# A fused attention and LayerNorm kernel: P times V in halves on neighbouring batches, a ring of eight units, scores copied in front of the transposition, LayerNorm's scale and shift on VectorE

## The chip, the cores and the metric

The kernel runs on one core of a Trainium2 chip. The metric is device time in microseconds of one launch that handles all 16 images. The engines are TensorE (PE; PEld is its weight load), VectorE (DVE), ScalarE (ACT), GpSimd (POOL) and SyncE (SP), which issues most transfers.

## The reference, cut to what matters

```python
x_seq = x.reshape(16, 900, 512)                # 16 images of 30 x 30 positions, float32
q, k, v = x_seq @ w + b                        # each split into 8 heads of 64 columns
scores = einsum('bhqd,bhkd->bhqk', q, k) / 8 + spatial_bias[|dh| + |dw|]
attn = softmax(scores)
ctx = einsum('bhqk,bhkd->bhqd', attn, v)       # back to (16, 900, 512)
resid = ctx @ wo + bo + x_seq
out = (resid - mean) * rsqrt(var + 1e-5) * gamma + beta
```

The bias depends only on the distance in the grid. The data are float32 throughout.

## The kernel before, in words

**Units.** A head pair (two heads of 64 columns, 128 partitions) is one of four per image. A *unit* is 60 queries (two rows of the grid) of one pair against all 900 keys: 15 units in a pair, 60 in an image (`UNITS`). The 900 keys lie as two halves of 450 on different partitions, so a unit is a tile of 128 partitions (4 blocks of 30 queries, padded to 32) by 2 heads by 450.

**What happens to a unit u.** Every engine's program is written out by hand as `body(im, u)`, run for u = 0 to 59 of each image in turn (`images`), and every engine runs strictly in that order. In the text "body 30" is an engine's instructions for u = 30. TensorE does its work in *batches* of two units, at even u.
- TensorE, batch u: the scores of units u+6 and u+7 (`scores`, L670; `AHEAD` is 6), into two PSUM places, one for even and one for odd units. The scores of a unit wait until the unit two before has been copied out.
- DVE, `biased_scores` (L919), in body u for unit u+6: adds the bias, finds the row minimum (the query weights are negated), and writes the result to `prob`, a ring of `RING` units in SBUF.
- ACT, `exponentials` (L787), body u, unit u+6: the exponential in place, with the row sum.
- SP, `exchange` (L474): in each odd body, four small transfers bring the minima and sums of the other half of the keys. It first waits until the exponential of the pair of units is done; the issues of this body that follow it on SP's queue (`keep_value`, stores, loads) stand behind that wait.
- POOL, `leads` (odd bodies) and `totals` (even bodies), with ACT's `ratios` (L795) between: the two halves are combined to one weight per query. ACT, `normalise` (L803), body u, unit u+2: probabilities times this weight.
- DVE, `turn` (L932), body u, unit u: a transposition of 32 by 32 blocks into `prob_t`, which holds two *groups* of up to four units. A pair has groups of 4, 4, 4 and 3 units; an image has 16 (g = 0 to 15).
- TensorE, `context` (L689): P times V of a group, 15 key blocks of four matmuls, accumulated in `pv_ps`, of which there is only one. The batches at which the groups run are `PV_UNITS`. ACT, `keep_context` (L813), copies the result out; the next group's P times V waits for that (`ctx_kept`).

**The background work.** In the same batches TensorE does the projections, whose float32 operands are split in a high and a low part and multiplied in three products. `SEQUENCE` lists the items in order: `piece` (p, j) is half of the keys or the queries of pair p (j = 0, 1 keys, 2, 3 queries; p = 4 and 5 are pairs 0 and 1 of the next image), `out` t is a tile of 120 tokens of the previous image times `wo`, `xt` t the transposition of a tile of the next image's x, `value` t a tile of its values. An item has four *steps* (three matmuls each), an `xt` one. `place` deals them out: so many steps to each batch, 4 where the batch has a P times V and 6 where not, until the list is at an end. It also sets the body in which each item is copied out (`EVICT`). Items alternate between two PSUM banks, so an item waits until the last but one before it has been copied out; `piece` and `value` by ACT (L743, L761), `xt` by ACT and then DVE (L730, L904), `out` by DVE.

**The end of an out tile.** POOL adds the bias to the residual (`add_bias`, L1056, one body ahead). DVE's `out_sum` adds it to the product and takes mean and variance (L943, L945, L947). POOL's `reciprocal_std` gives 1/std a body later (L1062, L1065); `out_norm` on DVE (L954) subtracts and scales in one instruction two bodies after the sum; `scale_shift` on POOL (L1072, L1074) then multiplies with gamma and adds beta; SP stores. `split_context` on POOL (L1044, L1046) splits the left operand of an out tile. The last image's out tiles (`final`) come at `FINAL_UNITS`, the last four behind the last attention work.

**Loads.** ACT issues the loads of the values of a pair (`LOADS`: body, pair and quarter; L777). The first one for the next image waits until all eight value tiles of that image are in memory (`v_kept`), which SP writes in `keep_value` (L466) one body after ACT staged them.

```python
LOADS = {..., 50: (4, 0), 52: (4, 1), 54: (4, 2), 56: (4, 3)}
def body(im, u):                 # vector
    if im.live(u):
        turn(im, u)
    if im.live(u + AHEAD):
        biased_scores(im, u + AHEAD)
```

## Time and profile before

| | us |
|---|---|
| median of 3 runs (lowest, highest) | 3438.34 (3435.63, 3443.45) |
| the profiled execution | 3438.66 |
| its span, first to last instruction | 3436.8 |
| busy: PE | 3164.5 (92%) |
| busy: ACT | 2781.2 (81%) |
| busy: DVE | 2557.5 (74%) |
| busy: POOL | 1683.3 (49%) |
| mean granted TensorE clock, share of full speed | 0.977 |

The profiled execution is 0.3 us over the median. Between the span and its time lie 1.9 us. The busy times are unions over the span; a matmul counts as busy also where it runs at half the clock. The chain that ended last is made up of PE 37%, POOL 18%, ACT 17%, DVE 15%, DMA 5% and small parts.

### The profile page before, as it was taken

What the parts mean: (1) busy time and instruction counts of PE and PEld (TensorE: products, weight loads), DVE (VectorE), ACT (ScalarE), POOL (GpSimd) and SP (SyncE); (2) the same over time, 40 slices, a digit from 0 to 9 for tenths busy, and PEclk for the clock granted to TensorE, in tenths of its full rate; (3) what the DMA queues carried; (4) which work ended last, traced back from release to release, by engine and by line L of the source; (5) the groups of instructions that cost most, each with busy time, mean ns of one, the idle gap of its engine ahead of it and who ended that gap; (6) DMA issues with size and microseconds to landing.
All of it is one profiled execution on the core that took longest, in us unless ns stands there. A gap on an engine that the chain in (4) does not pass through costs nothing.

```text
span 3436.8 us, 127113 instructions
## 1 busy us (share of the span) xinstructions
PE 3164.5 (92%) x52744; PEld 2150.3 (63%) x52744; DVE 2557.5 (74%) x5461; ACT 2781.2 (81%) x7015; POOL 1683.3 (49%) x3305
## 2 busy tenths in 40 slices
PE   3899999999999999999999999999999999999986
PEld 2566666666666666666666666666666666666654
DVE  2577878777787777878777786877778777786875
ACT  2698787888878888787888978888797888878783
POOL 0124627355372644727355372644627355372647
PEclk7999999999999999999999999999999999999998
DMA  5232322323232232322323232232322323232220
GB/s 153 64 83 61 93 77 61 95 61 95 69 86 80 68 93 61 93 76 62 95 61 96 68 89 77 69 92 66 89 81 66 90 57 96 66 89 77 69 64 23
DMA packets 317939, 267.44 MB, mean 78 GB/s; under 512 B 109913, under 2 KB 240985, under 8 KB 317361
## 3 DMA queue, kind: packets, MB, share of 16 engines
q1 hardware_dynamic: 172242, 130.32, 14.5%
q10 hardware_dynamic: 145120, 129.00, 12.4%
q8 instruction: 415, 6.80, 0.8%
q14 instruction: 162, 1.33, 0.1%
HBM read 193.73 MB, written 63.66 MB: 75 GB/s over the span
## 4 chain that ended last, share of the span: by engine, by line
PE 37%; POOL 18%; ACT 17%; DVE 15%; DMA 5%; SPq 4%; issue 3%; ACTq 0%; DVEq 0%; POOLq 0%
PE pv_ps L689 10%; PE s_ps L670 9%; ACT prob L787 7%; PE r_ps L587 7%; PE r_ps L605 7%; ACT prob L803 6%; DVE prob L919 5%; DMA other<-own 5%; POOL tokens L1072 4%; POOL tokens L1074 4%; DVE prob_t L932 4%; SPq L474 3%; POOL tokens L1056 2%; POOL weight L1029 2%; DVE stats L945 2%
## 5 line engine op out<-in xcount | busy, mean ns | idle before, releaser
L919 DVE CUSTOM_DVE_ANT_0 prob<-s_ps,window 128x450 f32<-128x450 f32 x1920 | 1126.7, 625 | 586.3 <-PE s_ps L670 490.9
L787 ACT ACTIVATE prob<-prob,own 128x450 f32<-128x450 f32 x1920 | 1266.1, 662 | 298.1 <-DVE own L919 295.7
L803 ACT ACTIVATE prob<-prob,weight 128x450 f32<-128x450 f32 x1920 | 1172.1, 659 | 80.0 <-POOL weight L1029 80.0
L932 DVE STREAM_TRANSPOSE prob_t<-prob 128x960 f32<-128x960 f32 x960 | 1124.4, 1171 | 62.4 <-ACT prob L803 54.9
L670 PE MATMUL s_ps<-k_sb,q_sb 64*32 64x450 f32 x15360 | 864.2, 552 | 85.5 <-DVE own L919 84.2
L689 PEld LDWEIGHTS pv_ps<-prob_t,values 64*64 64x64 f32 x30720 | 769.2, 136 | 227.6 <-issue 169.8
L689 PE MATMUL pv_ps<-prob_t,values 64*64 64x120 f32 x30720 | 824.9, 263 | 29.2 <-ACT ctx_sb L813 26.4
L587 PE MATMUL r_ps<-xt,w_sb 128*128 128x450 f32 x3072 | 710.1, 378 | 16.4 <-ACT q_sb L743 10.6
L587 PEld LDWEIGHTS r_ps<-xt,w_sb 128*128 128x128 f32 x3072 | 565.3, 190 | 153.6 <-issue 74.3
L1015 POOL TENSOR_TENSOR lead<-own,other 128x4 f32<-128x4 f32 x480 | 96.7, 201 | 913.1 <-DMA other<-own 912.9
L670 PEld LDWEIGHTS s_ps<-k_sb,q_sb 64*32 64x32 f32 x15360 | 228.4, 106 | 480.7 <-issue 304.2
L1029 POOL TENSOR_TENSOR weight<-total,minus_one 128x4 f32<-128x4 f32 x480 | 496.5, 1034 | 37.6
L605 PE MATMUL r_ps<-wv_sb,xt 128*120 128x512 f32 (+1 forms) x1536 | 389.6, 403 | 41.5 <-DVE wv_sb L888 38.5
L630 PE MATMUL r_ps<-wo_sb,ctx_split 128*120 128x512 f32 x1536 | 396.8, 405 | 15.7 <-POOL ctx_split L1046 8.3
L1024 POOL TENSOR_TENSOR total<-ratio,other 128x4 f32<-128x4 f32 x480 | 98.3, 205 | 588.1 <-ACT ratio L795 561.5
L787 ACT ACTIVATION_READ_ACCUMULATOR prob<-prob,own 128x1 f32 x1920 | 362.1, 189 | 0.0
L630 PEld LDWEIGHTS r_ps<-wo_sb,ctx_split 128*120 128x120 f32 x1536 | 271.2, 183 | 140.9 <-issue 57.9
L605 PEld LDWEIGHTS r_ps<-wv_sb,xt 128*120 128x120 f32 (+1 forms) x1536 | 261.1, 176 | 138.4 <-issue 58.9
L1072 POOL TENSOR_TENSOR tokens<-tokens,gamma_all 120x512 f32<-120x512 f32 x120 | 155.1, 1292 | 95.6 <-DVE tokens L954 95.5
L795 ACT ACTIVATE ratio<-lead 128x4 f32<-128x4 f32 x480 | 93.7, 195 | 97.7 <-POOL lead L1018 96.5
L919 DVE DVE_READ_ACCUMULATOR2_ANT own<- 128x1 f32 x1920 | 159.0, 83 | 0.0
L1074 POOL TENSOR_TENSOR tokens<-tokens,beta_all 120x512 f32<-120x512 f32 x120 | 154.2, 1285 | 9.4
(58 smaller groups left out, 1630.2 us busy)
## 6 DMA issues: line engine op xcount, KB each, us to landing
w_sb<-w_split ACTq DMA_DIRECT2D x126, 512.0 KB, 4.1
values<-v_dram ACTq DMA_DIRECT2D x256, 240.0 KB, 3.1
tokens<-in_x SPq DMA_DIRECT2D x214, 240.0 KB, 3.5
other<-own SPq DMA_DIRECT2D x1920, 1.0 KB, 2.1
out<-tokens SPq DMA_DIRECT2D x105, 240.0 KB, 3.0
v_dram<-stage SPq DMA_DIRECT2D x96, 240.0 KB, 2.8
v_dram<-stage SPq DMA_DIRECT2D x32, 180.0 KB, 2.5
tokens<-in_x SPq DMA_DIRECT2D x30, 120.0 KB, 3.2
```

Source lines behind the costliest of these rows:

```text
L587: last = pe.matmul(r_ps[:, bank, 0:HALF], w_sb[:, kind, a, k, :], xt[:, c, k, columns(half)], start=(k == 0 and i == 0), stop=(k == KT - 1 ...
L605: last = pe.matmul(r_ps[0:n, bank, :], xt[:, a, k, at:at + n], wv_sb[:, c, k, :], start=(k == 0 and i == 0), stop=(k == KT - 1 and i == PA ...
L630: last = pe.matmul(r_ps[0:TT, bank, :], ctx_split[:, t % 2, a, k, :], wo_sb[:, c, k, :], start=(k == 0 and i == 0), stop=(k == PAIRS - 1 a ...
L670: last = pe.matmul(s_ps[row:row + QUAD, u % 2, head, 0:HALF], q_sb[d, p % 2, q0:q0 + QUAD], k_sb[d, p % 2, columns(r)], start=True, stop=T ...
L689: last = pe.matmul(pv_ps[d, a, 0:n * GRID].rearrange("d (u w) -> d u w", u=n), values[half, p % 2, j, d], prob_t[half, g % 2, 0:n, head, Q ...
L787: nc.scalar.activation(prob[:, u % RING, head, 0:HALF], prob[:, u % RING, head, 0:HALF], ACT.Exp, scale=-1.0, bias=own[:, s, 0, c:c + 1], ...
L803: nc.scalar.activation(prob[:, u % RING, head, 0:HALF], prob[:, u % RING, head, 0:HALF], ACT.Copy, scale=weight[:, s, c:c + 1]).then_inc(p ...
L919: nc.vector.tensor_tensor_reduce(prob[:, u % RING, head, 0:HALF], s_ps[:, u % 2, head, 0:HALF], window[:, w0:w0 + HALF // GRID, :].rearran ...
L932: nc.vector.transpose(out=prob_t[:, g % 2, v % PER_GROUP, :, :].rearrange("p h k -> p (h k)"), in_=prob[:, u % RING, :, :].rearrange("p h ...
L1029: nc.gpsimd.tensor_tensor(weight[:, s, :], total[:, s, :], minus_one[:, :], ALU.pow).then_inc(weight_done, 1)
L1072: nc.gpsimd.tensor_tensor(y, y, gamma_all[0:m, :], ALU.mult).then_inc(scaled, 1)
L1074: nc.gpsimd.tensor_tensor(y, y, beta_all[0:m, :], ALU.add).then_inc(shifted, 1)
```

## The change

- `RING` 6 becomes 8, `STATS` 3 becomes 4, and both are indexed by the running number of the unit over all images, since 60 units are not a multiple of 8 (the renamed indices are left out below but for one).
- A group's P times V runs in two parts: key blocks 0 to 7 at its batch, 8 to 14 in the next batch. Groups 7 and 15 run whole, at batches 32 and 62 (62 being batch 2 of the next image), where they were at 30 and 60. `keep_context` moves from the end of ACT's body to the place in front of the exponentials.
- The steps per batch are now 5, 4 where a group starts in the first 16 units, 3 at batches 2 and 32 and 2 at 30 and 58. `piece` (1, 2) of the next image is done at the end of the image before it (and in the prologue), and `value` 7 comes after pair 4's pieces. The last loads of values go from bodies 50 to 56 to bodies 55 to 59.
- DVE copies the scores of u+6 in front of the transposition of u.
- LayerNorm: DVE's `out_sum` gets a fourth instruction, (y - mean) * gamma, and `out_norm` is (y * rstd) + beta; POOL's two instructions go, and its `add_bias` runs a body earlier.

```diff
@@ -35,23 +35,32 @@
 KEY, QUERY = 0, 1
 PIECES = [(KEY, 0), (KEY, 1), (QUERY, 0), (QUERY, 1)]
 AHEAD = 6
-RING = 6
-STATS = 3
+RING = 8
+STATS = 4
 SLOTS = 4
 END = UNITS + 10
-PV_UNITS = [4, 8, 12, 16, 20, 24, 28, 30, 34, 38, 42, 46, 50, 54, 58, 60]
-SPLIT_UNITS = [0, 0, 4, 7, 8, 11, 14, 16]
+PV_UNITS = [4, 8, 12, 16, 20, 24, 28, 32, 34, 38, 42, 46, 50, 54, 58, 62]
+PV_CUT = 8
+SPLIT_UNITS = [0, 0, 4, 6, 8, 11, 14, 17]
 LOAD_X = [22, 22, 25, 28]
-LOADS = {3: (1, 0), 5: (1, 1), 7: (1, 2), 9: (1, 3), 19: (2, 0), 21: (2, 1), 23: (2, 2), 25: (2, 3),
-         33: (3, 0), 35: (3, 1), 37: (3, 2), 39: (3, 3), 50: (4, 0), 52: (4, 1), 54: (4, 2), 56: (4, 3)}
-FINAL_UNITS = [54, 54, 58, 58, 62, 62, 64, 64]
-
-
-def group_at(u):
-
-    return {at: g for g, at in enumerate(PV_UNITS)}.get(u)
+LOADS = {5: (1, 0), 7: (1, 1), 9: (1, 2), 11: (1, 3), 21: (2, 0), 23: (2, 1), 25: (2, 2), 27: (2, 3),
+         35: (3, 0), 37: (3, 1), 39: (3, 2), 41: (3, 3), 55: (4, 0), 57: (4, 1), 58: (4, 2), 59: (4, 3)}
+FINAL_UNITS = [56, 56, 60, 60, 62, 62, 64, 64]
+
+
+def pv_parts(u, last=False):
+
+    parts = []
+    for g, at in enumerate(PV_UNITS):
+        whole = at in (32, 62) or last and g >= GROUPS - 2
+        at = min(at, UNITS) if last else at
+        if at == u:
+            parts.append((g, 0, BLOCKS if whole else PV_CUT))
+        elif at + 2 == u and not whole:
+            parts.append((g, PV_CUT, BLOCKS))
+    return parts
 def pieces(p, js=range(4)):
...
@@ -70,13 +79,23 @@
     return ("xt", t)
-SEQUENCE = [("piece", 1, 2), out(0), ("piece", 1, 3), out(1), out(2), out(3), ("piece", 2, 0), out(4), ("piece", 2, 1),
-            out(5), ("piece", 2, 2), out(6), ("piece", 2, 3), out(7)] + pieces(3)
+SEQUENCE = [("piece", 1, 3), out(0), out(1), out(2), out(3), ("piece", 2, 0), out(4), ("piece", 2, 1), out(5),
+            ("piece", 2, 2), out(6), ("piece", 2, 3), out(7)] + pieces(3)
 SEQUENCE += [xt(0), xt(1)]
 for tile in range(NT - 2):
     SEQUENCE += [value(tile), xt(tile + 2)]
-SEQUENCE += [value(NT - 2), value(NT - 1)] + pieces(4) + pieces(5, (0, 1))
-PV_STEPS, FULL_STEPS = 4, 6
+SEQUENCE += [value(NT - 2)] + pieces(4) + [value(NT - 1)] + pieces(5, (0, 1, 2))
+
+
+def room_at(u):
+
+    if u in (2, 32):
+        return 3
+    if u == UNITS - 2:
+        return 2
+    if u == 30:
+        return 2
+    return 4 if u < 16 and u % 4 == 0 else 5
 def steps(item):
@@ -90,22 +109,22 @@
         k = 0
         while k < steps(item):
             if not room:
-                cap = PV_STEPS if u in PV_UNITS or u == 0 else FULL_STEPS
-                u, room, used = u + 2, cap, 0
+                u, room, used = u + 2, room_at(u), 0
             n = min(room, steps(item) - k)
             at.setdefault(u - 2, []).append((item, k, k + n))
             k, room, used = k + n, room - n, used + n
         e = u - 2
-        ends[item] = min(e + (1 if cap == FULL_STEPS and used <= KT else 2), UNITS - 1)
+        ends[item] = min(e + (1 if used <= 2 or item[0] in ("xt", "out") else 2), UNITS - 1)
+    assert max(at) < UNITS
     return at, ends
 STEPS, EVICT = place(SEQUENCE)
 XT_UNITS = [u for tile in range(NT) for u in STEPS for w in STEPS[u] if w[0] == xt(tile)]
 BANK = {item: n % 2 for n, item in enumerate(SEQUENCE)}
-PROLOGUE = [("first_xt", t) for t in range(NT)] + pieces(4) + [value(t) for t in range(NT)] + pieces(5, (0, 1)) + [("bv_wo", 0)]
+PROLOGUE = [("first_xt", t) for t in range(NT)] + pieces(4) + [value(t) for t in range(NT)] + pieces(5, (0, 1, 2)) + [("bv_wo", 0)]
 PROLOGUE_STEPS = {-6: [value(0), value(1), value(2)], -4: [value(3), value(4), value(5)],
-                  -2: [value(6), value(7)] + pieces(5, (0, 1)) + [("bv_wo", 0)]}
+                  -2: [value(6), value(7)] + pieces(5, (0, 1, 2)) + [("bv_wo", 0)]}
 def bank_of(item):
...
+    def parts(self, u):
+
+        before = [] if self.first else [(Before(self), *part) for part in pv_parts(u + UNITS)]
+        return before + [(self, *part) for part in pv_parts(u, self.last) if u < UNITS or self.last]
...
@@ -467,7 +490,7 @@
             def exchange(im, x):
-                s = x // 2 % STATS
+                s = im.unit(x) // 2 % STATS
                 sp.wait_ge(exp_done, 2 * im.unit(x + 2))
...
@@ -653,7 +676,7 @@
                     of = pro if im.first and u == 0 else im
                     for bank in range(BANKS):
-                        mine = pieces(PAIRS if of is pro else p, (2, 3) if p == 1 else range(4))
+                        mine = pieces(PAIRS if of is pro else p, (3,) if p == 1 else range(4))
                         mine = [of.use(use) + 1 for use in mine if bank_of(use) == bank]
                         if mine:
...
-            def context(im, g):
+            def context(im, g, j0, j1):
                 p, gi = divmod(g, PAIR_GROUPS)
                 n, group = group_units(g), im.group(g)
-                pe.wait_ge(turned, im.unit(PER_PAIR * p + PER_GROUP * gi + n))
-                if gi == 0:
-                    pe.wait_ge(v_in[p % 2], 64 * (PAIRS // 2 * im.b + p // 2 + 1))
-                if not known(group):
-                    pe.wait_ge(ctx_kept, group)
-                for j in range(BLOCKS):
+                if j0 == 0:
+                    pe.wait_ge(turned, im.unit(PER_PAIR * p + PER_GROUP * gi + n))
+                    if gi == 0:
+                        pe.wait_ge(v_in[p % 2], 64 * (PAIRS // 2 * im.b + p // 2 + 1))
+                    if not known(group):
+                        pe.wait_ge(ctx_kept, group)
+                for j in range(j0, j1):
                     for a in range(2):
                         half = slice(2 * QUAD * a, 2 * QUAD * a + 2 * QUAD)
@@ -690,7 +714,8 @@
                                              values[half, p % 2, j, d],
                                              prob_t[half, g % 2, 0:n, head, QUAD * j:QUAD * j + GRID],
                                              start=(j == 0), stop=(j == BLOCKS - 1), skip_group_check=True)
-                last.then_inc(pv_full, 1)
+                if j1 == BLOCKS:
+                    last.then_inc(pv_full, 1)
             pe.wait_ge(ident_ok, 1)
             for t in range(NT):
                     return
-                if u == 0 and not im.first:
-                    context(Before(im), GROUPS - 1)
-                g = group_at(u)
-                if g is not None:
-                    context(im, g)
+                for of, g, j0, j1 in im.parts(u):
+                    context(of, g, j0, j1)
                 for work in im.background(u):
                     work_on(im, work[:-2], *work[-2:])
...
@@ -780,27 +802,27 @@
             def exponentials(im, u):
-                s = u // 2 % STATS
+                s = im.unit(u) // 2 % STATS
                 for head in range(2):
                     c = u % 2 * 2 + head
                     act.wait_ge(scores_min, 2 * im.unit(u) + head + 1)
-                    nc.scalar.activation(prob[:, u % RING, head, 0:HALF], prob[:, u % RING, head, 0:HALF], ACT.Exp,
+                    nc.scalar.activation(prob[:, im.unit(u) % RING, head, 0:HALF], prob[:, im.unit(u) % RING, head, 0:HALF], ACT.Exp,
                                          scale=-1.0, bias=own[:, s, 0, c:c + 1], accum_out=own[:, s, 1, c:c + 1]
                                          ).then_inc(exp_done, 1)
...
@@ -838,6 +860,9 @@
                         keep_piece(im, *work[1:])
                     elif work[0] == "value":
                         stage_value(im, work[1])
+                for of, g, j0, j1 in im.parts(u - 1):
+                    if j1 == BLOCKS:
+                        keep_context(of, g)
                 if im.live(u + AHEAD):
                     exponentials(im, u + AHEAD)
                 if u % 2 and im.live(u + 3):
@@ -860,11 +885,6 @@
                         load_values(im, 0, i)
                 if u in LOADS and not (im.last and LOADS[u][0] == PAIRS):
                     load_values(im, *LOADS[u])
-                if u == 1 and not im.first:
-                    keep_context(Before(im), GROUPS - 1)
-                g = group_at(u - 1)
-                if g is not None:
-                    keep_context(im, g)
             images(act, body)
...
@@ -910,14 +930,14 @@
                 unit, v = im.unit(u), u % PER_PAIR
-                s, w0 = u // 2 % STATS, WIN - HALF // GRID - 2 * v
+                s, w0 = im.unit(u) // 2 % STATS, WIN - HALF // GRID - 2 * v
                 dve.wait_ge(scores_full, unit + 1)
                 if not known(unit, RING - 1):
                     dve.wait_ge(turned, unit + 1 - RING)
                 for head in range(2):
                     c = u % 2 * 2 + head
                     nc.vector.tensor_tensor_reduce(
-                        prob[:, u % RING, head, 0:HALF], s_ps[:, u % 2, head, 0:HALF],
+                        prob[:, im.unit(u) % RING, head, 0:HALF], s_ps[:, u % 2, head, 0:HALF],
                         window[:, w0:w0 + HALF // GRID, :].rearrange("p a c -> p (a c)"),
                         1.0, BIG, ALU.add, ALU.min, own[:, s, 0, c:c + 1]).then_inc(scores_min, 1)
...
@@ -945,14 +965,17 @@
                 nc.vector.bn_stats(stats[0:m, i, :], y).then_inc(stats_done, 1)
                 dve.wait_ge(stats_done, n)
                 nc.vector.bn_aggr(mean_var[0:m, i, :], stats[0:m, i, :]).then_inc(mean_done, 1)
+                dve.wait_ge(mean_done, n)
+                nc.vector.scalar_tensor_tensor(out=y, in0=y, scalar=mean_var[0:m, i, 0:1], in1=gamma_all[0:m, :],
+                                               op0=ALU.subtract, op1=ALU.mult).then_inc(centred, 1)
             def out_norm(im, work):
-                t = work[1]
-                i, m, n = t % SLOTS, rows(t), out_no(im, work) + 1
-                y = y_of(t, work[0] == "final")
+                t, n = work[1], out_no(im, work) + 1
+                i, m, y = t % SLOTS, rows(t), y_of(t, work[0] == "final")
+                dve.wait_ge(centred, n)
                 dve.wait_ge(rstd_done, n)
-                nc.vector.tensor_scalar(y, y, mean_var[0:m, i, 0:1], rstd[0:m, i:i + 1],
-                                        ALU.subtract, ALU.mult).then_inc(normed, 1)
+                nc.vector.scalar_tensor_tensor(out=y, in0=y, scalar=rstd[0:m, i:i + 1], in1=beta_all[0:m, :],
+                                               op0=ALU.mult, op1=ALU.add).then_inc(shifted, 1)
             for t in range(NT):
                 xt_lo(pro, t)
@@ -969,10 +992,10 @@
             dve.wait_ge(cleared, 3)
             def body(im, u):
+                if im.live(u + AHEAD):
+                    biased_scores(im, u + AHEAD)
                 if im.live(u):
                     turn(im, u)
-                if im.live(u + AHEAD):
-                    biased_scores(im, u + AHEAD)
                 if u < 0:
                     if u == -3:
...
@@ -1065,16 +1088,6 @@
                 nc.gpsimd.tensor_tensor(rstd[0:m, i:i + 1], var_eps[0:m, i:i + 1], minus_half[0:m, :], ALU.pow
                                         ).then_inc(rstd_done, 1)
-            def scale_shift(im, work):
-                t, n = work[1], out_no(im, work) + 1
-                m, y = rows(t), y_of(t, work[0] == "final")
-                pool.wait_ge(normed, n)
-                nc.gpsimd.tensor_tensor(y, y, gamma_all[0:m, :], ALU.mult).then_inc(scaled, 1)
-                pool.wait_ge(scaled, n)
-                nc.gpsimd.tensor_tensor(y, y, beta_all[0:m, :], ALU.add).then_inc(shifted, 1)
-
-            pool.wait_ge(small_in, 16 * 3)
-
             def body(im, u):
                 if u % 2 == 0 and im.live(u + 2):
                     totals(im, u + 2)
@@ -1085,11 +1098,9 @@
                         use = ("bv_wo", 0)
                         pool.wait_ge(bank_free[bank_of(use)], pro.use(use) + 1)
                     return
-                for work in im.out_tiles(u - 2):
-                    scale_shift(im, work)
                 for work in im.out_tiles(u - 1):
                     reciprocal_std(im, work)
-                for work in im.out_tiles(u + 1):
+                for work in im.out_tiles(u + 2):
                     add_bias(im, work)
                 for t in range(NT):
...
@@ -1103,7 +1114,7 @@
 class Before:
     def __init__(self, im):
-        self.b, self.first = im.b - 1, False
+        self.b, self.first = im.b - 1, im.b == 1
```

## Rows read from the trace of the kernel before

**Rows 1.** The page, part 1: busy us (share of the span) and instructions by engine

```profile
PE 3164.5 (92%) x52744; PEld 2150.3 (63%) x52744; DVE 2557.5 (74%) x5461; ACT 2781.2 (81%) x7015; POOL 1683.3 (49%) x3305
```

**Rows 2.** Windows: us, busy PE, PEld, DVE, ACT, POOL, granted clock, DMA

```profile
400.00:3200.00 2800.00, 2666.06 (x44888) 1810.77 (x44886) 2152.53 (x4616) 2360.78 (x5970) 1405.97 (x2775) 0.99 0.28 79
1137.70:1149.00 11.30, 9.24 (x184) 6.75 (x188) 6.87 (x15) 9.44 (x25) 8.26 (x15) 0.85 0.03 5
...
1161.90:1204.60 42.70, 41.00 (x644) 27.32 (x642) 36.00 (x77) 30.74 (x78) 37.27 (x58) 1.00 0.29 82
```

**Rows 3.** Chain in order of time: the same pieces in two images, eight apart

```profile
1105.54 3.86 PE r_ps L587 x18
...
2750.04 3.86 PE r_ps L587 x18
```

**Rows 4.** Timeline of PE, batches 58 and 0: start, us, what, [idle before <-releaser]

```profile
1131.11 0.99 PE L670 MATMUL s_ps<-k_sb,q_sb 64*32 64x450 f32 x16 [0.59 <-DVE own L919]
1133.53 0.99 PE L670 MATMUL s_ps<-k_sb,q_sb 64*32 64x450 f32 x16 [1.43 <-DVE own L919]
...
1141.72 4.12 PE L689 MATMUL pv_ps<-prob_t,values 64*64 64x90 f32 x120 [1.93 <-ACT ctx_sb L813]
```

**Rows 5.** Timeline of PE, other batches

```profile
1116.90 1.74 PE L670 MATMUL s_ps<-k_sb,q_sb 64*32 64x450 f32 x32
1118.57 3.95 PE L587 MATMUL r_ps<-xt,w_sb 128*128 128x450 f32 x18
...
1124.12 3.31 PE L689 MATMUL pv_ps<-prob_t,values 64*64 64x120 f32 x120
1127.36 1.49 PE L587 MATMUL r_ps<-xt,w_sb 128*128 128x450 f32 x6
...
1150.16 3.05 PE L630 MATMUL r_ps<-wo_sb,ctx_split 128*120 128x512 f32 x12
...
1247.48 0.63 PE L562 MATMUL r_ps<-ident,tokens 120*128 120x120 f32 x4 [2.04 <-ACT q_sb L743]
```

**Rows 6.** Waits between 400 and 3200 us: total, times, longest

```profile
PE s_ps L670 <- DVE own L919: 55.9, 57, 2.4
...
DVE tokens L943 <- POOL tokens L1056: 72.1, 53, 2.6
```

**Rows 7.** Timeline of DVE: an out tile and the units beside it

```profile
1194.12 0.69 DVE L943 TENSOR_TENSOR tokens<-r_ps,tokens 120x512 f32<-120x512 f32 x1 [0.30 <-POOL tokens L1056]
...
1195.67 1.16 DVE L932 STREAM_TRANSPOSE prob_t<-prob 128x960 f32<-128x960 f32 x1
...
1198.08 1.17 DVE L932 STREAM_TRANSPOSE prob_t<-prob 128x960 f32<-128x960 f32 x1
```

**Rows 8.** Groups by line, DVE: busy us, mean ns, idle us before

```profile
L954 DVE TENSOR_SCALAR tokens<-tokens,mean_var,rstd 120x512 f32<-120x512 f32 x120 | 76.6, 638 | 5.3 <-POOL rstd L1065 5.3
...
L888 DVE SCALAR_TENSOR_TENSOR w_sb<-prob,w_sb 128x512 fp32r<-128x512 f32 x2 | 1.4, 682 | 5.5 <-ACT w_sb L725 5.5
```

**Rows 9.** Line 954, DVE: duration ns minimum/median/maximum

```profile
L954 DVE TENSOR_SCALAR tokens<-tokens,mean_var,rstd x120: 513/543/1366, 336.4 to 3293.7; 120x512 f32<-120x512 f32 x105, 60x512 f32<-60x512 f32 x15
```

**Rows 10.** The page, parts 5 and 6: normalisation, exchange and value stores (us to landing)

```profile
L803 ACT ACTIVATE prob<-prob,weight 128x450 f32<-128x450 f32 x1920 | 1172.1, 659 | 80.0 <-POOL weight L1029 80.0
...
v_dram<-stage SPq DMA_DIRECT2D x96, 240.0 KB, 2.8
```

**Rows 11.** Line 474, SP: duration of an issue, minimum/median/maximum ns

```profile
L474 SPq DMA_DIRECT2D other<-own x1920: 507/591/1856, 84.5 to 3377.6; - x192
```

**Rows 12.** The end: PE timeline, then groups between 3397 and 3437 us

```profile
3394.69 2.56 PE L689 MATMUL pv_ps<-prob_t,values 64*64 64x90 f32 x120
...
3412.85 7.15 PE L630 MATMUL r_ps<-wo_sb,ctx_split 128*120 128x512 f32 x24 [3.93 <-POOL ctx_split L1046]
...
L1072 POOL TENSOR_TENSOR last_tokens<-last_tokens,gamma_all 120x512 f32<-120x512 f32 (+1 forms) x6 | 7.8, 1305 | 4.3 <-DVE last_tokens L954 4.3
L1074 POOL TENSOR_TENSOR last_tokens<-last_tokens,beta_all 120x512 f32<-120x512 f32 (+1 forms) x6 | 7.7, 1279 | 0.5
```

21 lines of the change are left out of this document (10 added, 11 removed).

## The prediction, made before the changed kernel was run

> **What bounds the kernel now.** First the page's busy times: PE is busy for 92% of the span, no other engine for more than 81% [rows 1]. So the question is what the 8% are, and where. The windows take them out of the steady part: between 400 and 3200 us PE is busy for 2666.1 of 2800 us, 133.9 idle [rows 2]. The same piece of the chain lies at 1105.54 and, eight images later, at 2750.04 us [rows 3], so an image takes 1644.5/8 = 205.6 us and the window holds 13.6 images: 9.8 us of idle PE in each. The granted clock there is 0.99 [rows 2], which is 28 us of full-speed time, some 2.1 us an image. In all 11.9 us of an image are lost, and 193.7 are matmuls at full speed. Nothing in the change removes a matmul, so 11.9 us an image is the most that it can give in the steady part.
>
> Where they lie: the timeline of PE shows, at the end of an image, gaps of 0.59, 1.43 and 1.93 us [rows 4]. Batch 56 has neither background steps nor a P times V, batch 58 only a P times V: the list ran out at batch 54. PE then outruns the minima on DVE (4.8 us for two units against 1.7 of scores) and waits, and group 15, two units behind group 14, waits for `pv_ps`. In the window around this the clock is 0.85 over 11.3 us [rows 2]: part of it is at 1.2 instead of 2.4 GHz, right behind these thin batches, for 1.7 us. That is 5.7 us. At batch 28, `xt` 1 wants the bank of a `piece` that ACT copies out only in body 30: 2.04 us [rows 5]. What is left of 9.8, 3.8 us, is small waits: some 1.2 us, three times 0.4, for an `xt` bank, and some 2.6 us in batches 4 to 24, where the waits for the minima (55.9 us in the window [rows 6]) mostly fall, and where DVE itself waits 72.1 us, 5.3 an image, for POOL's bias [rows 6].
>
> **The change, part by part.**
>
> *Levelled batches.* Start to start, the scores of two units take 1.67 us, a P times V 3.24 (2.5 with three units), 18 matmuls of `piece`, six steps, 3.88 (0.65 a step), 12 of `out` 2.95 (0.74 a step, taken for `value` too), an `xt` 0.6 [rows 5]. Before, the batches go 1.67 + 3.24 + 4 x 0.74 = 7.9 and 1.67 + 6 x 0.65 = 5.5 in turn, at the end 6.2, 1.7, 4.9. Now I deal the list out by the new rule: batch 6 is 1.67 + 1.51 (7 of 15 blocks) + 5 x 0.74 = 6.9, and so on; all lie between 6.1 and 6.9 but for 5.8 (batch 0), 4.7 (58) and 4.5 (30). Both schedules sum to 192.0. The three gaps and the clock's fall at the end of the image go (5.7), `xt` 1 moves to batch 30, where its bank has been free for 2 us (2.0), and each `xt` has a batch of its own (1.2). Cover: ACT needs 2360.8/409 = 5.8 us for two units with all its copies [rows 2]; the three thin batches are each followed by full ones, and a ring of eight carries them.
>
> *The cut itself.* A run of `piece` behind a P times V costs 1.49 for 6 matmuls where a run of 18 has 1.32 for 6 [rows 5]: a start costs up to 0.17. There are 14 more runs of P times V: 0 to 2.4 us. Scores followed by P times V show no gap, so I take 0.5. `keep_context`, 0.35 us, now stands in front of ACT's exponentials and holds them back by that; ACT has the room. With the second half at batch u+2 and the next group at u+4, it has some 3 us in hand.
>
> *Scores in front of the transposition.* DVE's work is the same. The minimum that PE waits for is done one transposition earlier behind an out tile's work, but a group's first half finds its last unit turned later: where DVE is late, 0.6 us an image. The ring of eight only makes this order possible.
>
> *LayerNorm on DVE.* A unit takes DVE 2.41 us (1195.67 to 1198.08), an out tile 1.55 for sum, statistics and aggregation (1194.12 to 1195.67) [rows 7] and 0.54 for the scaling [rows 9]. Now the aggregation is waited out (0.1) and two three-operand instructions of 512 columns follow; such a one took 0.68 [rows 8], 0.72 with its start: 1.55 + 0.1 + 1.44 = 3.1 a tile, 1.0 more. Tiles are evicted in bodies 5, 7, 7, 9, 13, 17, 19, 23. Batches 6 to 24 are 65.4 us of PE. DVE needs 20 x 2.41 + 8 x 3.1 = 73.0: 7.6 us more. So DVE is the bound of this stretch. It can be late: PE asks for the second minimum of a batch 6.5 + 0.9 us after the start of the one before, and DVE has it after 4.4, so 3.0 us are absorbed, and 4.6 reach PE, most of it at batches 10 to 12, behind body 7 with its two tiles. Collisions: the scaling has a median of 543 ns but a mean of 638 and a maximum of 1366 [rows 8, 9], so now and then something holds it for 0.8 us. No row shows what does that to an instruction with two SBUF tensors. Bounds: nothing, and 0.8 on each of 16 (13 us). I take what the scaling has, 0.1 each, as the nearest row: 1.5, of which 1.2 counts. This stretch costs 4.6 + 0.6 + 1.2 = 6.4 us, against 2.6 before.
>
> *POOL.* It loses 2.6 us a tile, so the bias comes in time, and DVE's 5.3 us of waiting go; the 73.0 above hold none.
>
> *Value 7 and the loads.* ACT stages `value` 7 in body 54; SP writes it in body 55, behind the exchange that waits for the exponential of unit 61, that is four issues of 0.59 [rows 11], its own, and 2.8 to landing [rows 10]: 5.8 us behind that exponential. ACT's first load of values in body 55 waits for it, two normalisations (1.2 us [rows 10]) behind the same exponential. ACT stands still for 4.6 us, and with it exponentials 62 and on. Batches of 6.4 us against ACT's 5.8 and the 3 us in hand cover most of it. Bounds 0 and 4.6; I take 1.0.
>
> *Ends.* Behind the last attention work POOL is the chain: between 3397 and 3437 us the two lines that go are 15.5 of 40 us [rows 12], and more of them stand just ahead. DVE adds 1.5: 18 us less, between 5 and 25. The prologue gets a `piece` more, 3 us at the mixed clock; image 0 has room for its loss only.
>
> **Sum.** Per image 0.5 + 6.4 + 1.0 = 7.9 us stay lost of 11.9: 4.0 less. There are 15 ends of images and 15 stretches of out tiles: 60 us. With 18 - 3: 75 us. 3438.7 of the profiled execution (0.3 over the median) minus 75 is 3364.
>
> **Rivals.**
> - *DVE's work stays hidden.* It has 25% idle overall [rows 1], and before, with 8 x 2.1 + 5.3 of waiting, its stretch was also long, and PE lost 2.6. Then 3 us stay lost: 8.9 x 15 + 15 = 149 less, 3290. Against: 73.0 over 65.4.
> - *The hole on ACT decides.* All 4.6 reach PE: 3.6 more an image, 3418; if the clock falls with it as it does now, 1.7 more, 3443. For: this wait is new, and the thin batch 58 comes right behind. Against: ACT is never the last releaser for long today.
> - *Slower: the two new DVE instructions collide with POOL.* POOL is busy in 37.3 of the 42.7 us of the out stretch [rows 2] and keeps over half of that. If each takes the 1.37 us of the longest scaling [rows 9], a tile takes 1.65 + 2.74 + 0.1 = 4.5, the stretch 84.2; 15.8 reach PE, 17.9 in all stay lost, 6.0 more than now: +90 - 15, 3514. It decides from 1.1 us for each of the two. Against: only a small part of the scalings collide. The Trainium skill (GPSIMD Engine Reference, Key points) says that POOL's SBUF interfaces are shared with VectorE, with contention for DVE instructions in a two-port mode or with two SBUF inputs. By that rule the two new ones are open to it as the scaling is, where the sum and the statistics are not.
> - *It does not do what it says:* the lost time only spreads, since other engines pace PE all along: 3438. Against: each gap in rows 4 and 5 has its own cause in the dealing.
>
> **How the numbers follow.** Forecast 60%, DVE hidden 15%, ACT's hole 12%, slower 9%, no change 4%. A measurement of this kernel tells 0.2% from no change (6.9 us). Faster: 60 + 15 + 8 of the 12 = 83%; within: 4 + 3 = 7%; slower 10% (1 of the 12 and 9). The range runs from the hidden case, 3290, to 3425, where the collisions or ACT's hole cost 4 us an image more than I take; the slower case is left out.
>
> **What would show it.** Right: no gaps at batches 56 to 0 and no clock below 1.00 there; no wait of `xt` for ACT; PE's waits for DVE's minima gathered where the out tiles are, at 5 to 7 us an image; L943's wait for POOL gone; an ACT wait for the value store of 4 to 5 us once an image; a tail some 18 us shorter; an image of about 201.6 us. Wrong: the new instructions' means above 0.9 us; the clock's falls still there; PE waiting for `ctx_sb` at every group, which would say that the halves leave ACT no time.

## The result and the profile after

The changed kernel took 3301.64 us (median of 4 runs, 3300.54 to 3303.32) against 3440.89 for the kernel before beside it: ratio 0.9602, 95% interval 0.9585 to 0.9619. It is 139 us faster, where 75 were forecast. Ratios go by the kernel before run beside each; one execution of `turn_first`, the profiled one, took 5927.8 us at a lower granted clock and is left out.

The page of the changed kernel, span and part 1 (to [rows 1]):

```profile
span 3299.0 us, 127110 instructions
PE 3141.2 (95%) x52744; PEld 2127.7 (64%) x52744; DVE 2608.9 (79%) x5589; ACT 2758.5 (84%) x7015; POOL 1413.7 (43%) x3049
```

Its window between 400 and 3200 us (columns as in [rows 2]):

```profile
400.00:3200.00 2800.00, 2749.72 (x46602) 1863.32 (x46601) 2285.77 (x4917) 2426.31 (x6189) 1243.19 (x2680) 1.00 0.30 81
```

To compare images, the same work at the same place of the schedule serves as a mark: the first scores of batch 0, in images 1 and 15, in the timeline of PE. Kernel before, then changed kernel:

```profile
311.85 0.99 PE L670 MATMUL s_ps<-k_sb,q_sb 64*32 64x450 f32 x16
...
3198.85 0.98 PE L670 MATMUL s_ps<-k_sb,q_sb 64*32 64x450 f32 x16
```

```profile
308.19 1.74 PE L693 MATMUL s_ps<-k_sb,q_sb 64*32 64x450 f32 x32
...
3079.80 1.74 PE L693 MATMUL s_ps<-k_sb,q_sb 64*32 64x450 f32 x32
```

Fourteen images take 2887.0 us before (206.2 each) and 2771.6 after (198.0 each): 115.4 us less. From the last mark to the end of the span it is 238.0 and 219.2, 18.8 less, and 3.7 less lie ahead of the first. That is the whole difference of the spans, 137.8 us. In the window, 14.1 images by the new pace, PE is idle for 50.3 us, 3.6 an image for 9.8, and the granted clock is 1.00 for 0.99: of 11.9 us lost per image, 3.6 are left.

The end of an image, timeline of PE (to [rows 4]):

```profile
1094.35 1.74 PE L693 MATMUL s_ps<-k_sb,q_sb 64*32 64x450 f32 x32
1096.02 1.87 PE L713 MATMUL pv_ps<-prob_t,values 64*64 64x120 f32 x64
1097.82 1.48 PE L610 MATMUL r_ps<-xt,w_sb 128*128 128x450 f32 x6
1099.23 1.74 PE L693 MATMUL s_ps<-k_sb,q_sb 64*32 64x450 f32 x32
1100.90 1.67 PE L713 MATMUL pv_ps<-prob_t,values 64*64 64x120 f32 x56
1102.50 2.74 PE L610 MATMUL r_ps<-xt,w_sb 128*128 128x450 f32 x12
```

Batches 58 and 0: no gap is left, and none for `xt` 1 but 0.4 us. The two halves take 1.80 and 1.60 us where one piece took 3.24 [rows 5].

Waits of the changed kernel between 400 and 3200 us (to [rows 6]):

```profile
ACT prob L825 <- POOL weight L1052: 66.1, 46, 3.0
ACT k_sb L765 <- issue: 61.9, 14, 5.9
...
POOL tokens L1079 <- DMA tokens<-in_x: 52.9, 14, 5.2
...
PE s_ps L693 <- DVE own L939: 32.3, 32, 1.5
DVE prob_t L952 <- PE pv_ps L713: 32.3, 29, 1.2
...
PE pv_ps L713 <- ACT ctx_sb L835: 7.4, 16, 4.0
```

PE's waits for minima are 32.3 us, 2.3 an image (55.9 before), nearly all of them at batches 10 and 12. ACT stands still once an image for 4.4 us: this is the first load of values, foreseen. DVE no longer waits for POOL's bias; instead POOL waits for the residual's load, which nobody feels.

DVE in the changed kernel, around an out tile (to [rows 7]) and, in the last two lines, a long one of the new instructions with what POOL does beside it:

```profile
1117.12 0.65 DVE L963 TENSOR_TENSOR tokens<-r_ps,tokens 120x512 f32<-120x512 f32 x1
...
1118.75 0.75 DVE L969 SCALAR_TENSOR_TENSOR tokens<-tokens,mean_var,gamma_all 120x512 f32<-120x512 f32 x1
1119.42 0.62 DVE L939 CUSTOM_DVE_ANT_0 prob<-s_ps,window 128x450 f32<-128x450 f32 x1
...
1120.51 1.17 DVE L952 STREAM_TRANSPOSE prob_t<-prob 128x960 f32<-128x960 f32 x1
1121.61 0.59 DVE L939 CUSTOM_DVE_ANT_0 prob<-s_ps,window 128x450 f32<-128x450 f32 x1
...
1122.67 1.17 DVE L952 STREAM_TRANSPOSE prob_t<-prob 128x960 f32<-128x960 f32 x1
...
1125.40 1.70 DVE L969 SCALAR_TENSOR_TENSOR tokens<-tokens,mean_var,gamma_all 120x512 f32<-120x512 f32 x1
```

```profile
1125.33 1.22 POOL L1069 TENSOR_TENSOR ctx_split<-ctx_sb,ctx_split 128x480 fp32r<-128x480 f32 x1
```

A unit takes DVE 2.16 us (1120.51 to 1122.67) where it took 2.41: the next copy starts 1.10 us after a transposition starts and not 1.31 (1195.67 to 1196.98 in the kernel before, whose copy is shown with the first experiment). The four instructions of an out tile take 2.30 us (1117.12 to 1119.42). The new instructions by line, minimum/median/maximum:

```profile
L969 DVE SCALAR_TENSOR_TENSOR tokens<-tokens,mean_var,gamma_all x120: 742/752/1850, 327.6 to 3162.8; 120x512 f32<-120x512 f32 x105, 60x512 f32<-60x512 f32 x15
```

```profile
L977 DVE SCALAR_TENSOR_TENSOR tokens<-tokens,rstd,beta_all x120: 698/747/1810, 338.3 to 3167.8; 120x512 f32<-120x512 f32 x105, 60x512 f32<-60x512 f32 x15
```

### The profile page after: what moved, and what is told of

Same layout as the page of the kernel before. It is cut to its first block and busy times, and to the rows that moved or that the text cites. A ratio compares the mean times of both kernels' runs of the same rounds, so it can differ in the third digit from the quotient of the medians.

```text
span 3299.0 us, 127110 instructions
## 1 busy us (share of the span) xinstructions
PE 3141.2 (95%) x52744; PEld 2127.7 (64%) x52744; DVE 2608.9 (79%) x5589; ACT 2758.5 (84%) x7015; POOL 1413.7 (43%) x3049
## 5 line engine op out<-in xcount | busy, mean ns | idle before, releaser
L939 DVE CUSTOM_DVE_ANT_0 prob<-s_ps,window 128x450 f32<-128x450 f32 x1920 | 1108.3, 613 | 458.9 <-PE s_ps L693 458.8
L713 PEld LDWEIGHTS pv_ps<-prob_t,values 64*64 64x64 f32 x30720 | 752.5, 133 | 379.3 <-issue 335.8
L693 PE MATMUL s_ps<-k_sb,q_sb 64*32 64x450 f32 x15360 | 845.9, 544 | 43.8 <-DVE own L939 42.1
L713 PE MATMUL pv_ps<-prob_t,values 64*64 64x120 f32 x30720 | 856.2, 260 | 26.3 <-ACT ctx_sb L835 24.2
L1038 POOL TENSOR_TENSOR lead<-own,other 128x4 f32<-128x4 f32 x480 | 112.1, 233 | 1017.2 <-DMA other<-own 1016.8
L1047 POOL TENSOR_TENSOR total<-ratio,other 128x4 f32<-128x4 f32 x480 | 106.0, 221 | 661.2 <-ACT ratio L817 633.0
L1079 POOL TENSOR_TENSOR tokens<-tokens,bo_all 120x512 f32<-120x512 f32 x120 | 156.3, 1308 | 56.9 <-DMA tokens<-in_x 56.9
L939 DVE DVE_READ_ACCUMULATOR2_ANT own<- 128x1 f32 x1920 | 157.3, 82 | 0.0
L1069 POOL TENSOR_TENSOR ctx_split<-ctx_sb,ctx_split 128x480 fp32r<-128x480 f32 (+1 forms) x128 | 149.9, 1171 | 10.3
```

The costliest lines, as they stand in the source:

```text
L693: last = pe.matmul(s_ps[row:row + QUAD, u % 2, head, 0:HALF], q_sb[d, p % 2, q0:q0 + QUAD], k_sb[d, p % 2, columns(r)], start=True, stop=T ...
L713: last = pe.matmul(pv_ps[d, a, 0:n * GRID].rearrange("d (u w) -> d u w", u=n), values[half, p % 2, j, d], prob_t[half, g % 2, 0:n, head, Q ...
L939: nc.vector.tensor_tensor_reduce(prob[:, im.unit(u) % RING, head, 0:HALF], s_ps[:, u % 2, head, 0:HALF], window[:, w0:w0 + HALF // GRID, : ...
L1069: nc.gpsimd.tensor_tensor(ctx_split[:, t % 2, 1, :, 0:m], src, ctx_split[:, t % 2, 0, :, 0:m].bitcast(F32), ALU.subtract).then_inc(split_l ...
L1079: nc.gpsimd.tensor_tensor(y, y, bo_all[0:rows(t), :], ALU.add).then_inc(res_bias, 1)
```

## The experiments

The last two columns are read from the one profiled execution of each kernel: the length of an image between the marks used above, and what lies behind the last mark.

| kernel | what | median us | ratio to before (95%) | image us | behind us |
|---|---|---|---|---|---|
| before | | 3440.9 | 1 | 206.2 | 238.0 |
| changed | | 3301.6 | 0.960 (0.9585 to 0.9619) | 198.0 | 219.2 |
| ring7 | changed, ring of 7 | 3315.7 | 0.963 (0.9604 to 0.9662) | 199.0 | 218.5 |
| turn_first | changed, transposition first | 3384.9 | 0.983 (0.9795 to 0.9866) | | |
| turn_first_again | the same kernel | 3380.7 | 0.982 (0.9797 to 0.9844) | 203.1 | 223.2 |
| ln_pool | changed, scale and shift on POOL | 3384.7 | 0.983 (0.9809 to 0.9847) | 202.9 | 233.1 |
| whole | changed, P times V whole | 3370.9 | 0.979 (0.9766 to 0.9811) | 201.9 | 220.1 |
| write_first | changed, value written before the exchange | 3299.1 | 0.959 (0.9556 to 0.9613) | 198.0 | 219.2 |
| before_ring8 | before, ring of 8 | 3415.5 | 0.992 (0.9893 to 0.9946) | 204.8 | 235.2 |
| before_ln | before, scale and shift on DVE | 3446.3 | 1.002 (1.0001 to 1.0032) | 207.6 | 222.2 |
| level_only | before, halves and dealing | 3469.4 | 1.007 (1.0055 to 1.0093) | 208.4 | 235.4 |
| old_batches | before, all but halves and dealing | 3419.5 | 0.994 (0.9919 to 0.9952) | 206.3 | 222.5 |
| out2_later | changed, tile 2 ends a body later | 3303.8 | 0.960 (0.9590 to 0.9619) | 198.1 | 220.2 |
| spread | changed, pieces between the out tiles | 3275.1 | 0.952 (0.9505 to 0.9534) | 196.2 | 219.0 |

**The transposition's own signal.** After the result the DVE rows asked for a cause: the copy of unit u+6 into a ring of six waits for `turned` of unit u, which stands directly in front of it; with a ring of eight it waits for an older one. The copy in the kernel before, behind the transposition of 1195.67 [rows 7]:

```profile
1196.98 0.63 DVE L919 CUSTOM_DVE_ANT_0 prob<-s_ps,window 128x450 f32<-128x450 f32 x1
```

A ring of seven in the changed kernel brings that wait back, since there the copy stands in front of the transposition of u and behind that of u-1:

```diff
-RING = 8
+RING = 7
```

> The changed kernel with a ring of 7 units for 8. The copy of the scores of unit u+6 then reuses the place of unit u-1, whose transposition stands directly in front of it on DVE, so its wait ends only when that transposition has signalled. Theory A (this wait costs DVE some 0.2 us a unit, which the ring of eight removes, and that is why the out tiles' stretch stayed hidden): the distance from a transposition to the next copy goes from 1.1 back to 1.3 us, PE's waits for the minima grow by 3 to 5 us an image, 3345 to 3380 us. Theory B (DVE's work is the same in either ring and the levelled batches alone hide it): within 5 us of the changed kernel's 3301.6.

The timeline of DVE with a ring of seven:

```profile
1120.78 1.18 DVE L952 STREAM_TRANSPOSE prob_t<-prob 128x960 f32<-128x960 f32 x1
1122.09 0.63 DVE L939 CUSTOM_DVE_ANT_0 prob<-s_ps,window 128x450 f32<-128x450 f32 x1
```

The 1.31 us are back, where a ring of eight has 1.10 (1120.51 to 1121.61): the wait on a signal just given costs 0.21 us a unit, 13 us of DVE an image. That part of theory A is shown. Its worth in time is small: PE's waits for minima go from 32.3 to 38.7 us, 0.5 us an image where A had 3 to 5, those of its weight loads from 82.4 to 103.6, the image is 1.0 us longer and the kernel 14 us slower by the medians, with intervals that overlap. In the changed kernel most of this DVE time is hidden, so of the surprise at most those 14 us are the ring's.

```diff
-RING = 6
+RING = 8
-prob[:, u % RING ...]
+prob[:, im.unit(u) % RING ...]
```

> The kernel before with a ring of 8 alone, places counted over all images. Theory A: transposition to copy falls from 1.31 to 1.1 us, DVE's work by 12 us an image; the part of PE's waits for minima that lies in the out tiles' stretch and at batches 56 and 58 shrinks, 1 to 3 us an image, 3395 to 3425 us. Theory B: within 7 us of the kernel before.

```profile
1118.10 1.18 DVE L932 STREAM_TRANSPOSE prob_t<-prob 128x960 f32<-128x960 f32 x1
1119.19 0.59 DVE L919 CUSTOM_DVE_ANT_0 prob<-s_ps,window 128x450 f32<-128x450 f32 x1
```

The distance is 1.09 us, and the kernel is 29 us faster, as A said: in a kernel where PE waits more for the minima (55.9 us against 32.3), the same 0.21 us pay twice as much.

**The order of copy and transposition.**

```diff
+                if im.live(u):
+                    turn(im, u)
                 if im.live(u + AHEAD):
                     biased_scores(im, u + AHEAD)
-                if im.live(u):
-                    turn(im, u)
```

> The changed kernel, ring of 8, with DVE's transposition of u again in front of the copy of the scores of u+6. Theory A (it is the place that is reused, not the order, that counts): transposition to copy stays at 1.1 us, time within 8 us of 3301.6. Theory C (the order itself gives the gain, because PE's minimum comes one transposition earlier): PE's waits for the minima grow by 1 to 3 us an image, 3315 to 3345 us.

Ratio 0.983, some 83 us slower than the changed kernel: more than either theory allowed, and without a profile that can be used. So the same kernel ran again with a new theory:

> The changed kernel with the transposition in front, as run before: it was some 85 us slower than the changed kernel, which neither theory A (no difference) nor the size of theory C (14 to 43 us) foresaw, and its profile was of a disturbed execution. Theory D, formed on that: the first transposition of a group waits for the P times V of the group two before (pv_full), whose second half now ends 1.6 to 3.2 us into the batch; in this order that wait stands in front of the copy of the scores, so the minimum and the exponentials come late, in the changed order behind it. Expected: 3375 to 3395 us again; DVE prob_t waiting for PE pv_ps as before in total (30 us between 400 and 3200) or more, but PE waiting for the minima by over 80 us (32 in the changed kernel). If it is theory C's mechanism (a minimum that comes one transposition later everywhere), these waits are spread evenly over all batches and prob_t's wait for pv_ps is no larger.

Waits of this run between 400 and 3200 us:

```profile
PEld s_ps L693 <- DVE own L939: 185.0, 183, 2.6
DVE prob_t L952 <- PE pv_ps L713: 144.3, 99, 3.1
...
DVE prob_t L952 <- ACT prob L825: 87.3, 114, 3.7
PE s_ps L693 <- DVE own L939: 86.5, 88, 2.2
```

And one place, PE and DVE:

```profile
1123.66 0.99 PE L693 MATMUL s_ps<-k_sb,q_sb 64*32 64x450 f32 x16 [0.16 <-DVE own L939]
1124.58 1.67 PE L713 MATMUL pv_ps<-prob_t,values 64*64 64x120 f32 x56
```

```profile
1126.39 1.18 DVE L952 STREAM_TRANSPOSE prob_t<-prob 128x960 f32<-128x960 f32 x1 [2.78 <-PE pv_ps L713]
1127.49 0.59 DVE L939 CUSTOM_DVE_ANT_0 prob<-s_ps,window 128x450 f32<-128x450 f32 x1
```

The transposition that opens a group may overwrite `prob_t` only when the P times V two groups back has ended. Its second half ends at 1126.2; the transposition has waited 2.78 us, and the copy of scores that are long there starts at 1127.49. In the changed order that copy goes first, and the wait behind it falls to 32.3 us in total. Theory D holds, in its waits (144.3, 86.5) and its time. The halves create this wait, for in the run `whole` below it is not in the list, and the order takes it off the path: the order is worth 79 us here. D is not all of it: the transposition also waits 87.3 us for ACT's normalisation (9.6 in the changed kernel), and that wait too stands in front of the copy now. How much of it is only a consequence of the late copies was not separated.

**LayerNorm's end.** What concerns it in the change, undone (the bias stays a body early):

```diff
-                nc.vector.scalar_tensor_tensor(out=y, ..., in1=gamma_all, op0=ALU.subtract, op1=ALU.mult)
...
+                nc.vector.tensor_scalar(y, y, mean_var[0:m, i, 0:1], rstd[0:m, i:i + 1], ALU.subtract, ALU.mult)
...
+                for work in im.out_tiles(u - 2):
+                    scale_shift(im, work)
```

> The changed kernel with LayerNorm's scale and shift back on POOL, all else as changed. Theory E (the move frees more than it costs: DVE's waits for POOL's bias and the tail): DVE waits for the bias again by 3 to 6 us an image, the tail is 15 to 20 us longer, 3320 to 3350 us. Theory F (the move overloads DVE where the out tiles are, and PE's remaining waits for minima are its price): these waits fall below 10 us between 400 and 3200, the steady part gains 1 to 2 us an image and the tail loses what E says, 3290 to 3310 us.

Waits between 400 and 3200 us, then POOL, ACT and PE at one place:

```profile
ACT prob L826 <- POOL weight L1049: 245.7, 117, 4.1
...
PE pv_ps L714 <- ACT ctx_sb L836: 82.5, 30, 5.7
```

```profile
756.64 1.26 POOL L1094 TENSOR_TENSOR tokens<-tokens,beta_all 120x512 f32<-120x512 f32 x1
...
758.42 1.04 POOL L1049 TENSOR_TENSOR weight<-total,minus_one 128x4 f32<-128x4 f32 x1
```

```profile
759.50 1.23 ACT L826 ACTIVATE prob<-prob,weight 128x450 f32<-128x450 f32 x2 [4.13 <-POOL weight L1049]
760.63 0.35 ACT L836 ACTIVATE ctx_sb<-pv_ps 128x240 f32<-128x240 f32 x1
```

```profile
761.12 3.48 PE L714 MATMUL pv_ps<-prob_t,values 64*64 64x120 f32 x64 [5.56 <-ACT ctx_sb L836]
```

83 us slower, beyond both theories. The tail is 13.9 us longer, near E's 15 to 20, but E's place in the image is wrong: DVE waits for the bias only 1.3 us in all. It is POOL's queue: four scale and shift instructions in a row, 5.1 us, stand in front of a weight; ACT's normalisation waits 4.13 us for that, the copy of `ctx_sb` stands behind it, and PE waits 5.56 us for the copy. Such waits sum to 82.5 us of the 92.3 us that PE is idle between 400 and 3200 us, some 6 us an image, and the granted clock there is 0.98 where the changed kernel has 1.00. DVE stands behind the same queue: its scaling waits 90.7 us for POOL's 1/std, up to 4.8 us at a time.

```diff
+                dve.wait_ge(mean_done, n)
+                nc.vector.scalar_tensor_tensor(out=y, ..., in1=gamma_all, op0=ALU.subtract, op1=ALU.mult)
...
-                for work in im.out_tiles(u - 2):
-                    scale_shift(im, work)
```

> The kernel before with LayerNorm's scale and shift on DVE and the bias a body earlier, nothing else. Theory I (POOL's two instructions delay the weights, and ACT's copy of ctx_sb only matters where the halves make it tight): ACT's wait for the weight falls from 70 us between 400 and 3200 to below 40, but the image hardly changes, since here DVE's copies wait for the transposition's signal; the tail gives 10 to 20 us: 3415 to 3435 us. Theory J (the move is worth its 80 us of the undoing run by itself): 3350 to 3375 us.

Alone the move gives nothing: the ratio is 1.002 (1.0001 to 1.0032). I's gain of the tail came, 222.2 us behind the last mark for 238.0, and the images lost it again, 207.6 us for 206.2. ACT's wait for the weight is gone from the list, but DVE pays: ACT waits 377.6 us for minima (252.9 in the kernel before), PE 76.2 (55.9).

**Halves and dealing.**

```diff
-        whole = at in (32, 62) or last and g >= GROUPS - 2
+        whole = True
```

> The changed kernel with each P times V in one piece at its first batch, steps per batch as changed. A cut costs PE 0.16 us by the changed kernel's rows (1.80 + 1.60 against 3.24), 14 of them 2.2 us an image. Theory G (the halves level the batches, and that is worth more): batches of 8.2 and 5.0 us in turn bring back waits for minima and for ctx_sb, 2 to 6 us an image net of the 2.2: 3330 to 3400 us. Theory H (ring and order alone carry uneven batches): the 2.2 us come back, 3265 to 3290 us.

Theory G, 69 us. Window and waits between 400 and 3200 us:

```profile
400.00:3200.00 2800.00, 2698.32 (x45796) 1838.58 (x45798) 2242.61 (x4830) 2385.48 (x6084) 1234.18 (x2634) 0.99 0.29 80
```

```profile
ACT ctx_sb L835 <- POOL ctx_split L1069: 60.4, 13, 5.9
...
PE r_ps L585 <- ACT q_sb L765: 32.0, 14, 2.3
```

Part of it is this experiment's own: `keep_context` of group 3 now comes at body 17, where POOL splits tile 7, and ACT waits 4.6 us for that in each image. So 69 us, net of what the cut costs, is a bound from above for the halves. `xt` 1 waits again for its bank, 2.3 us an image, though the dealing is the changed one.

```diff
-RING = 8
+RING = 6
...
+                if im.live(u):
+                    turn(im, u)
...
+                for work in im.out_tiles(u - 2):
+                    scale_shift(im, work)
```

> Halves and new dealing alone: ring of 6, transposition in front, LayerNorm's end on POOL. By theory D the wait for the halves lies in front of the scores here too, and the transposition's own signal as well: 3400 to 3450 us, no or a small gain over the kernel before. If the levelling were worth by itself what my sum gave it (the end of the image 5.7 us, xt 1 2.0): 3340 to 3370 us.

25 us slower than the kernel before beside it by the medians, 0.7% by the ratio, even outside what D allowed. Both of the waits above are there at once, and the granted clock between 400 and 3200 us is 0.98, lower than before the change:

```profile
ACT prob L826 <- POOL weight L1049: 214.0, 121, 4.2
...
DVE prob_t L953 <- PE pv_ps L714: 138.1, 95, 2.8
```

The other way round, everything but halves and dealing (the edits of before_ring8 and before_ln together, and the copy in front):

> All of the change but the batches: ring of 8, scores in front, LayerNorm on DVE, with the old list, steps and whole P times V at the old places. Theory K (the parts only pay together; the end of the image, 5.7 us with the clock's fall, and xt 1, 2.0, are the dealing's alone): 3375 to 3410 us, with the gaps of batch 58 and 0 and of xt 1 still there. Theory L (the batches matter little once DVE and POOL are relieved): 3310 to 3340 us.

Only 0.65% (K had 1 to 2%), and all of it is tail: 222.5 us behind the last mark for 238.0, while the image takes 206.3 us for 206.2. The ring's 1.4 us an image (before_ring8) and the 1.4 that LayerNorm's move costs (before_ln) cancel. The gap of `xt` 1 stands as it was, and the clock in the window is 0.99; ACT's total stops for want of minima grew to 325.4 us.

**The hole on ACT.**

```diff
+                for work in im.evicted(u - 1):
+                    if work[0] == "value":
+                        keep_value(im, work[1])
                 if u % 2 and im.live(u + 5):
                     exchange(im, u + 5)
```

> The changed kernel with SP's write of a value tile in front of the exchange of the same body. ACT's stop of 4 to 6 us at the first load of values (14 times between 400 and 3200 us) should go. If that stop reaches PE, 0.5 to 1.5 us an image come back: 3280 to 3294 us. If the ring and the thin batch cover it, as the small idle time of PE behind batch 58 suggests: within 5 us of 3301.6.

The stop of ACT at the first load is gone from the waits, and the time stays within the noise. It is covered.

**What is left.** PE's idle time at batches 10 and 12 lies behind body 7, which ends two out tiles.

```diff
+EVICT[out(2)] = 8
```

> The changed kernel with out tile 2 ended by DVE in body 8 in place of body 7, which has two tiles now. PE's idle time at batches 8 to 12 (2 to 2.4 us an image) is put down to that pair: if so, it falls by 0.5 to 1.5 us an image, 3280 to 3295 us. If it comes from the three tiles in bodies 7 to 9 as a whole, which stay, within 5 us of 3301.6.

Nothing. Then the whole cluster:

```diff
-SEQUENCE = [("piece", 1, 3), out(0), out(1), out(2), out(3), ("piece", 2, 0), out(4), ("piece", 2, 1), out(5), ...
+SEQUENCE = [("piece", 1, 3), out(0), out(1), ("piece", 2, 0), out(2), out(3), ("piece", 2, 1), out(4), ("piece", 2, 2), out(5),
+            ("piece", 2, 3), out(6), ("piece", 3, 0), out(7)] + pieces(3, (1, 2, 3))
-LOAD_X = [22, 22, 25, 28]
+LOAD_X = [22, 24, 26, 30]
```

> The changed kernel with pieces dealt between the out tiles, which then end in bodies 5, 7, 9, 11, 15, 19, 21 and 25, no two in one, and the loads of x a little later. If the cluster of three tiles in bodies 7 to 9 is what DVE cannot hide, PE's waits for minima fall from 2.3 to below 1 us an image: 3270 to 3290 us. If DVE's total in this stretch is the bound, within 6 us of 3301.6.

3275.1 us, 26 us faster than the changed kernel, and the intervals are apart. Its window, and PE's weight loads waiting for minima (82.4 us in the changed kernel):

```profile
400.00:3200.00 2800.00, 2765.14 (x47087) 1874.92 (x47078) 2298.99 (x4967) 2448.22 (x6254) 1272.27 (x2704) 1.00 0.30 82
```

```profile
PEld s_ps L693 <- DVE own L939: 41.1, 66, 2.3
```

PE is idle for 34.9 us, 2.5 an image, and the image is 1.8 us shorter. It is the cluster of three tiles in bodies 7 to 9, not DVE's total, which is the same; but the last tile also ends two bodies later and the loads of x move, and neither was tried alone. This version beats both kernels.

## Why the prediction was right, and where it was not

**What bounds the kernel, and the most that the change can give.** Right. 11.9 us an image were lost; 8.2 came back, and the matmuls themselves took the same time: 2749.7/14.14 = 194.5 us an image against (2666.1 - 28)/13.58 = 194.3 at full speed.

**The levelled batches.** Right: the three gaps of the seam, the clock's fall and the wait of `xt` 1 are gone. But the sum booked this to the dealing alone, and level_only shows that halves and dealing by themselves lose 0.7%, at a clock of 0.98.

**The cut.** 0.5 us an image was taken; one group's two halves took 0.16 us more than one piece, which would be 2.2 an image for 14, but the whole of PE's full-speed work grew by 0.2 us. The run `whole` settles the price: with the same dealing and no cut, full-speed work is (2698.3 - 28)/13.87 = 192.5 us an image, 2.0 less. So the term was mis-sized by 1.5 us, inside its bound of 2.4. Why the kernel before, without a cut too, has 194.3 no run explains. What the halves cost elsewhere was left out: see the order of copy and transposition.

**Scores in front of the transposition: the step that failed.** It said "DVE's work is the same", a loss of 0.6 us an image, and "the ring of eight only makes this order possible". Two things were missed. The wait on the transposition's own signal in a ring of six, 0.21 us a unit, is inside the 2.41 us that I read from rows 7 as the work of a unit: the copy at 1196.98 starts 1.31 us after a transposition that lasts 1.16. And the wait for `pv_full` in front of a group's first transposition, 4.0 us in all in the kernel before, becomes 32.3 us in the changed kernel and 144.3 in the old order (1.5 us each time, up to 3.1). Keeping the copy in front of it is what the order is worth, 79 us, and the text has no word of it. I had looked who waits for DVE, not what DVE would wait for.

**LayerNorm on DVE.** The price was near: 2.30 + 0.67 us a tile (start to start) against 3.1, and the new instructions have a median of 0.75 us with a tail to 1.85. Their means, 0.89 and 0.86 us, lie 0.13 and 0.12 over the medians, where 0.1 each was taken, and just under the 0.9 that was to be a sign of being wrong. The stretch of the out tiles was the mis-sized term: 6.4 us an image were expected, and PE waits 2.3 us for minima in the whole image. The shorter unit explains part (20 x 0.25 = 5 us of DVE in the stretch), but with a ring of 7, where it does not apply, the waits are only 2.8 us an image (38.7/14). The reading that fits is that DVE makes up behind the stretch what it is late at its end, without PE feeling it, where the sum had charged nearly all beyond 3.0 us to PE; no run shows this directly. The rival of collisions with POOL, 3514 us, is refuted. The Trainium skill (GPSIMD Engine Reference, Key points) has contention with GpSimd for two SBUF inputs. The trace agrees: 53 of the 256 new instructions took over 0.1 us more than their median, and each of the 53 ran beside an addition of 480 or 512 columns on POOL (L1069, L1079; the last section has more). That POOL's relief would decide was not in the text: it counted the bias and the tail, and not the weight, on which ACT's copy and then PE hang.

**ACT's hole.** Its place and length were right (4.6 us said, 4.4 measured); its cost, 1.0 us an image, is nothing that can be measured.

**The ends.** 18.8 us less behind the last mark, of which an image's share is 8.2: 10.6 for the last image and tail, against 18. Ahead of the first mark 3 us more were expected, and it is 3.7 less. Together 14.3 against 15: two misses that cancel, which is luck.

**The sum.** 7.9 us an image were to stay lost, and 3.6 did: 4.3 x 15 = 64 us, which is all of the difference between 75 and 139. The 75 had the right bound and the right gaps, and missed the two terms that decide whether they can be closed: what the halves make the transposition wait for, and what POOL's queue makes ACT wait for. The time lies between the forecast and the rival "DVE's work stays hidden" (3290), nearer to the latter.

## What to carry to other kernels

Parts of a change of schedule are not a sum: here the halves, the order and LayerNorm's move cost 69 to 83 us each when undone, while by itself LayerNorm's move gave nothing, halves and dealing lost 25 us and only the ring gave something, 29. Without the halves the parts did add up (old_batches); it is with them that each of the others becomes necessary. When a step is moved or cut, list anew what each queue will wait for in its new place, own signals included, and what stands behind that wait. A distance between starts that is longer than the instruction (1.31 against 1.16 us here) may hold a wait and is worth a run, and clusters of extra work matter more than their total.
